# Moving the scaled down weights four steps earlier, the slot weight to VectorE, and swapping two waits in a fused attention and mixture-of-experts kernel

## The reference

```python
mod = (silu(c) @ wmod).reshape(2, 6, 1, 256)          # sa, ca, ga, sb, cb, gb
ga, gb = sign(ga) * max(|ga|, 0.25), sign(gb) * max(|gb|, 0.25)
h = layernorm(x) * (1 + ca) + sa
q, k, v, u = split(h @ W_qkvu.T); q, k = silu(q), silu(k)
o = decayed_linear_attention(q, k, v)                 # 16 heads of 16, a decay for each head
x = x + ga * ((u * rmsnorm(o)) @ W_out.T)
h = layernorm(x) * (1 + cb) + sb
# feed-forward: a shared expert, and the best 2 of 8 experts for each row
out = (silu(h @ sh_gate.T) * (h @ sh_up.T)) @ sh_down.T
for e in range(8):
    out += ((silu(h @ ex_gate[e].T) * (h @ ex_up[e].T)) @ ex_down[e].T) * comb[:, e]
x = x + gb * out
```

## Time and profile before

| | us |
|---|---|
| median of 3 runs | 419.76 (419.39 to 420.69) |
| the profiled execution | 419.39 |
| its span | 417.6 |
| TensorE busy | 391.2 |
| VectorE busy | 295.8 |
| ScalarE busy | 273.0 |
| GpSimd busy | 192.9 |

### The profile page before, as it was taken

How to read it: one execution, slowest core, us unless ns; L and a number is a source line. 1 busy time by engine, 2 the same in 40 slices (tenths; PEclk the granted TensorE clock), 3 DMA queues, 4 the chain that set the end, 5 groups by cost and what they waited for, 6 DMA issues and landing times.

```text
span 417.6 us, 11545 instructions
## 1 busy us (share of the span) xinstructions
PE 391.2 (94%) x4071; PEld 288.5 (69%) x4096; DVE 295.8 (71%) x601; ACT 273.0 (65%) x541; POOL 192.9 (46%) x192
## 2 busy tenths in 40 slices
PE   7989998999889867999999999999999999999993
PEld 4655466788668767999965666666666666666892
DVE  6996478898698763789778677767767775555542
ACT  4688667566666437475657778778687856656640
POOL 1000006577767964113445555565665565564240
PEclk9999999999999989899999999999999999999998
DMA  7850020001930069962322243344334333433224
GB/s 268 314 85 17 0 103 2 2 27 23 357 142 28 17 241 312 291 203 31 77 64 66 39 64 65 53 60 68 53 54 64 59 58 53 70 60 44 34 27 113
DMA packets 26253, 38.70 MB, mean 93 GB/s; under 512 B 4996, under 2 KB 20340, under 8 KB 26072
## 3 DMA queue, kind: packets, MB, share of 16 engines
q1 hardware_dynamic: 16120, 25.53, 19.3%
q0 software_dynamic: 7488, 10.27, 15.8%
q10 hardware_dynamic: 2592, 2.18, 1.6%
HBM read 27.60 MB, written 10.36 MB: 91 GB/s over the span
## 4 chain that ended last, share of the span: by engine, by line
PE 63%; DVE 17%; issue 7%; ACT 6%; DMA 4%; ACTq 1%; DVEq 1%; SPq 0%; POOLq 0%
PE ps L1508 23%; PE ps L1546 14%; PE ps L1516 8%; PE ps L1336 5%; PE ps L1525 4%; DVE wx L946 4%; PE ps L1479 3%; DMA wx<-in_wexp 2%; DVE xres L1009 2%; DVE tmp L1023 1%; DVE st L1012 1%; PE ps L1322 1%; DMA tmp<-in_decay_tables 1%; DVE rs L1041 1%; DVE st L862 1%
## 5 line engine op out<-in xcount | busy, mean ns | idle before, releaser
L1508 PE MATMUL ps<-wx,tmp 128*128 (+1 forms) x448 | 103.0, 379 | 1.1
L540 POOL DMA_INDIRECT out<-tmp,dk x39 | 66.2, 1699 | 70.7 <-DMA out<-tmp,dk 57.5
L1546 PE MATMUL ps<-wx,tmp 128*128 (+1 forms) x660 | 80.9, 273 | 0.2 <-DVE tmp L1193 0.2
L774 ACT ACTIVATE tmp<-tmp 128x512 bf16<-128x512 f32 x55 | 34.6, 629 | 63.3 <-DVE tmp L1184 37.3
L1508 PEld LDWEIGHTS ps<-wx,tmp 128*128 128x128 bf16 x468 | 44.2, 98 | 46.0
L1546 PEld LDWEIGHTS ps<-wx,tmp 128*128 128x128 bf16 x660 | 63.8, 98 | 16.0 <-DVE tmp L1193 0.5
L533 POOL DMA_INDIRECT tmp<-h2rows,src_i x39 | 41.4, 1061 | 20.9 <-issue 9.8
L1516 PE MATMUL ps<-tmp,wx 128*128 128x128 bf16 x768 | 48.9, 225 | 1.5 <-ACT tmp L765 1.5
L1199 DVE SCALAR_TENSOR_TENSOR woutg<-modr,w_hl,woutg 128x256 f32<-128x256 f32 x39 | 18.9, 485 | 42.7 <-ACT woutg L783 42.7
L1516 PEld LDWEIGHTS ps<-tmp,wx 128*128 128x128 bf16 x768 | 46.6, 101 | 1.8 <-issue 1.7
L1193 DVE TENSOR_TENSOR tmp<-tmp 128x512 bf16<-128x512 f32 x55 | 38.7, 704 | 6.8 <-ACT tmp L774 6.6
(11 more groups left out here) (195 smaller groups left out, 704.6 us busy)
## 6 DMA issues: line engine op xcount, KB each, us to landing
wx<-in_wexp SPq DMA_DIRECT2D x27, 512.0 KB, 5.5
xres<-in_x SPq DMA_DIRECT2D x4, 512.0 KB, 8.2
h2rows<-h2s ACTq DMA_DIRECT2D x16, 128.0 KB, 3.6
out<-h2s SPq DMA_DIRECT2D x12, 128.0 KB
h2s<-in_wmod SPq DMA_DIRECT2D x1, 1024.0 KB, 9.3
wx<-decay_rows SPq DMA_DIRECT2D x16, 64.0 KB
modr<-mod_rows SPq DMA_DIRECT2D x1, 1024.0 KB, 4.7
wx<-in_wqkvu SPq DMA_DIRECT2D x1, 768.0 KB, 8.4
```

Of the source, the lines that this page charges most:

```text
L540: e.indirect_dma_start(t["out"], bass.IndirectOffsetOnAxis(ap=dst_i[:, j:j + 1], axis=0), yb[(NA + j) % 2], None, compute_op=ALU.add).then ...
L774: e.activation(hs[p][:, 0:FF], hf[p], ACT.Copy).then_inc(s["inner_high"], 1)
L1508: ins = e.matmul(ps[:, bank, :], xT[p][:, (2 * a + k) * P:(2 * a + k + 1) * P], wx[:, bass.ds(at_ + weights(part, w) + k * FF, FF)], start ...
L1546: ins = e.matmul(half(DOWN_BANKS[p], 0, D), inner[:, (KF * a + k) * P:(KF * a + k + 1) * P], wx[:, bass.ds(off, D)] if routed(f) else wx[: ...
```

## The change

Three things:

- The products of the down piece run at steps 10 to 13 instead of 14 to 17, the second batch's first (into the stage's first slot), then the first batch's in place. The splits of these two products are at steps 13 and 15 of ScalarE (low parts at 14 and 16 of VectorE) instead of 16 and 18 (17 and 19). The second batch's is now the third part and the first batch's the fourth, so that `down(0)` waits for all four low parts, and `down(1)` for none.
- `make_weight` leaves ScalarE. VectorE makes the slot weight in `take_rows`, right behind the copy of the turned rows.
- In `add_rows` the two waits stand in the other order.

```diff
--- before.py
+++ after.py
@@ -345,8 +345,8 @@
             return early_stage[:, stage * PIECE:(stage + 1) * PIECE], wx[:, at_[0]:at_[0] + PIECE], wx[:, at_[1]:at_[1] + PIECE]
 
         SHARED_PARTS = [shared_part(0, [SHARED_AT + weights(0, a) for a in range(2)]), shared_part(1, [SHARED_AT + weights(1, a) for a in range(2)]),
-                        shared_part(0, [SHARED_AT + weights(2, a) for a in range(2)]), shared_part(2, [SECOND_DOWN + a * PIECE for a in range(2)])]
-        SHARED_PARTS_AT = (9, 10, 16, 18)
+                        shared_part(0, [SECOND_DOWN + a * PIECE for a in range(2)]), shared_part(2, [SHARED_AT + weights(2, a) for a in range(2)])]
+        SHARED_PARTS_AT = (9, 10, 13, 15)
 
 
 
@@ -514,19 +514,19 @@
 
 
                 part = slice(part * PIECE // 2, (part + 1) * PIECE // 2)
-                down, other_ = early_stage[:, 2 * PIECE:3 * PIECE][:, part], early_stage[:, 0:PIECE][:, part]
-                if b == 0:
-                    e.wait_ge(s["shared_loaded"], 16 * NPIECE)
+                down, second = early_stage[:, 2 * PIECE:3 * PIECE][:, part], early_stage[:, 0:PIECE][:, part]
+                e.wait_ge(s["shared_loaded"], 16 * NPIECE)
+                if b == 1:
                     e.wait_ge(s["shared_low"], 1)
                 else:
-                    e.wait_ge(s["shared_scaled"], 2)
-                e.tensor_tensor((other_, down)[b].rearrange("p (k n) -> p k n", n=D), down.rearrange("p (k n) -> p k n", n=D),
+                    e.wait_ge(s["second_scaled"], 2)
+                e.tensor_tensor((down, second)[b].rearrange("p (k n) -> p k n", n=D), down.rearrange("p (k n) -> p k n", n=D),
                                 modr[:, b, 3:4, :].to_broadcast([P, KF // 2, D]), ALU.mult).then_inc(s[("shared_scaled", "second_scaled")[b]], 1)
 
             for n in range(N_IT):
                 step_attention(n)
-                if 14 <= n < 18:
-                    scale_down((n - 14) // 2, n % 2)
+                if 10 <= n < 14:
+                    scale_down(1 - (n - 10) // 2, n % 2)
 
             def gather(j):
                 wait(e, "weight_made", j - 1)
@@ -535,8 +535,8 @@
 
             def add_rows(j):
 
+                wait(e, "result_made", j + 1)
                 wait(e, "rows_added", 16 * j)
-                wait(e, "result_made", j + 1)
                 e.indirect_dma_start(t["out"], bass.IndirectOffsetOnAxis(ap=dst_i[:, j:j + 1], axis=0),
                                      yb[(NA + j) % 2], None, compute_op=ALU.add).then_inc(s["rows_added"], 16)
 
@@ -696,9 +696,9 @@
                     whole_, high, _ = SHARED_PARTS[SHARED_PARTS_AT.index(n)]
                     e.wait_ge(s["shared_loaded"], 16 * NPIECE)
                     if n == SHARED_PARTS_AT[2]:
+                        e.wait_ge(s["second_scaled"], 2)
+                    if n == SHARED_PARTS_AT[3]:
                         e.wait_ge(s["shared_scaled"], 2)
-                    if n == SHARED_PARTS_AT[3]:
-                        e.wait_ge(s["second_scaled"], 2)
                     e.activation(high, whole_, ACT.Copy).then_inc(s["shared_high"], 1)
                 if mine(l):
                     tile = tile_of(l)[0]
@@ -745,17 +745,6 @@
                     wait(e, "inner_turned", f - NA + 1)
                     wait(e, "down_product", f - 1)
                     e.activation(hsT[f % 2], ps[:, FREE_BANK, :].bitcast(bf16), ACT.Copy).then_inc(s["inner_taken"], 1)
-
-            def make_weight(f):
-
-                if is_tile(f) and routed(f):
-                    j = f - NA
-                    wait(e, "rows_turned", f + 1)
-                    if j == 0:
-                        e.wait_ge(s["routing"], RT_COLUMNS + 4)
-                    w = xg[f % 2][:, D:].bitcast(f32)
-                    e.activation(slot_w[:, j:j + 1], w[:, 1:2], ACT.Identity, scale=second[:, j:j + 1],
-                                 bias=w[:, 0:1]).then_inc(s["weight_made"], 1)
 
             def middle(f):
                 if is_tile(f):
@@ -821,7 +810,6 @@
             f = N_IT - NT - 1
             middle(f - 1)
             for f in range(f, NF + 3):
-                make_weight(f + 1)
                 take_inner(f - 2)
                 take_rows(f + 1)
                 if f == MARK_AT:
@@ -1172,6 +1160,11 @@
                     wait(e, "up_product", f - 1)
                     e.tensor_copy(xT[f % 2].bitcast(u32), half(ROW_BANK, 0, D).bitcast(u32)).then_inc(s["rows_taken"], 1)
 
+                    j = f - NA
+                    w = xg[f % 2][:, D:].bitcast(f32)
+                    e.scalar_tensor_tensor(out=slot_w[:, j:j + 1], in0=w[:, 1:2], scalar=second[:, j:j + 1], in1=w[:, 0:1],
+                                           op0=ALU.mult, op1=ALU.add).then_inc(s["weight_made"], 1)
+
             def make_inner(f):
                 if is_tile(f):
                     p = f % 2
@@ -1535,8 +1528,8 @@
                         e.wait_ge(s["expert_low"], NPIECE)
                 else:
                     wait(e, "inner_low", f + 1)
-                    if f < B:
-                        e.wait_ge(s["shared_low"], NPIECE + f)
+                    if f == 0:
+                        e.wait_ge(s["shared_low"], NPIECE + 1)
                 down_free(e, f)
                 for n in range(3 * KF):
                     k, (a, w) = n // 3, PASSES[n % 3]
```

## The result

The changed kernel takes 424.2 us (median of 9 runs, 422.62 to 426.1), the kernel before beside it 420.38 (9 runs, 418.76 to 422.29): ratio 1.0093, 95% interval [1.0064, 1.012]. It is about 0.9% slower. The forecast was 418.7 with a range of 416.0 to 421.5; the time lies outside.

The account below looks back on a forecast made before the run. TensorE was taken as the bound in the routed tiles, the hand-over from attention as the place to gain. 0.4 - 0.6 - 0.8 + 0 = -1.0 us gave 418.4, or 418.7 us as median; range 416.0 to 421.5.

Parts of the forecast that it names:

- Part C: Swapping the two waits of add_rows before the 39 chained adds: nothing, between -0.1 and +0.5 us.
- A: Shared down weights' products and splits four steps earlier in attention: net +0.4 us, between -2.0 and +3.4.
- the clock: TensorE's granted clock at the hand-over from attention to shared tiles: -0.6 us taken, bounds 0 and -3.4.
- three terms: Work added in steps 10 to 16: GpSimd lateness 1.6, products meeting L1041 0.6, copies and differences 2.1; 4.3 us.
- the meetings: GpSimd products (L523) and VectorE's L1041 excluding each other: 1.08 and 0.94 us removed in steps 15 and 16, 0.6 added.
- the copies: Two ScalarE copies leaving TensorE's path, in step 16 and at 161.45 us: 0.95 us gained each.
- Rival 3: Clock stays up over the hand-over: 2.5 us more gain than taken, near 416.2 us; chance 0.22.
- B at the first routed tiles: Near 221 us, slot weight off ScalarE lets L1193 run before the gather: -0.8 us, bounds -0.93 and +0.6.
- B in the steady ring: VectorE–ScalarE ring of the expert tiles: 39 added operations at 0.08 us each, covered by 0.40 us per four tiles; cost nothing.
- Rival 1: Ring of the expert tiles becomes the bound, deciding at 0.10 us per weight; 421.5 us at 0.2 us; chance 0.14.
- Part B: Slot weight moved from ScalarE to VectorE: free in steady tiles unless 0.21 us or more each, -0.8 us at the first.
- The shape of the end: Last two adds with the waits swapped: the next to last gains about 0.5 us, the last loses 0.5.

Follow-up runs that it names:

- A and B: Kernel before with down products and splits moved earlier and the slot weight made on VectorE, add_rows waits in their old order: 417.48 us, ratio 0.9939.
- A only: Kernel before with only the down weights' products moved to steps 10 to 13 and their splits to 13 and 15: 416.85 us, ratio 0.9914.
- products alone: Kernel before with the four GpSimd products at steps 10 to 13, the splits left where they were: 418.56 us, ratio 0.9943.
- filled idle: Kernel before with ten unused matmuls of 512 columns put where TensorE idled 2.75 us at the hand-over: 420.16 us, ratio 0.9988.
- A and B with the weight in the gap: Kernel before with down products and splits earlier, old wait order, slot weight on VectorE behind L1184, where VectorE waits for ScalarE: 417.06 us, ratio 0.9921.
- double weight: Kernel before with the slot weight made on VectorE, and the same operation once more into columns nobody reads: 424.61 us, ratio 1.0091.
- B alone: Kernel before with only the slot weight moved from ScalarE to VectorE, behind the copy of the turned rows: 420.81 us, ratio 1.001.

## Why the prediction was wrong

The step that failed is **Part C**, "Nothing, between -0.1 and +0.5". It had the mechanism right (the wait first in the text is the one to which the DMA reacts fast; 0.76 us against 0.24) and asked the wrong question of it. It looked at the last two adds of the kernel, where one gains 0.5 and one loses 0.5, and not at the 37 before them. In the changed kernel the landing of the add before is what ends the wait of 36 of the 39. For those the term is a period: transfer 3.87 plus reaction 0.75 is 4.62 us, against TensorE's 4.57. It was over the threshold, and no rival priced it. Measured: +5.5 us alone, +6.5 on top of A and B.

Point by point:

- **A, +0.4 us, range -2.0 to +3.4; with the clock -0.2.** Measured -3.6. The distances of L1006 (L994) from step to step, from the one at 111.90 us on (before) and its counterpart, show where, in us:

| | 1 | 2 | 3 | 4 | 5 | 6 | 7 | 8 |
|---|---|---|---|---|---|---|---|---|
| before | 6.24 | 5.86 | 5.29 | 5.29 | 5.03 | 6.28 | 6.23 | 6.54 |
| A only | 6.24 | 6.39 | 5.67 | 6.71 | 5.20 | 5.90 | 4.34 | 4.91 |
| products alone | 6.24 | 6.38 | 5.67 | 5.76 | 5.48 | 5.20 | 5.29 | 5.13 |
| filled idle | 6.24 | 5.87 | 5.28 | 5.29 | 5.02 | 6.28 | 6.23 | 5.84 |

What the work adds in its new steps is 2.5 us (columns 2 to 5: 0.53, 0.38, 1.42, 0.17), where the prediction summed 4.3 from three terms; 1.8 of it are the products. What it gives back in its old ones is 3.9 us (columns 6 to 8), and 2.4 more from the last residual to the first down: 6.3 where 4.5 was forecast (2.0 for the meetings, 1.9 for the copies, 0.6 for the clock). The clock is 0.7 us of column 8, as the kernel with the filled idle shows, which has that gain and no other, and 1.4 of the 2.4. So 4.2 us are meetings and copies, near the forecast 3.9. Two terms were mis-sized, to the same side: the added work by 1.8 us and the clock by 1.5. The prediction said "the work meets the same neighbours a little earlier"; in fact the same work cost 2.5 us in the middle steps and 4.2 in the last ones, where TensorE, ScalarE and the shared tiles' start all stand in a queue. VectorE's wait in step 7 shows it, 2.25 us for ScalarE before and 0.16 with A (a row of before, then of A alone):

```profile
152.12 0.16 DVE L1006 RECIPROCAL rs<-rs 128x1 f32<-128x1 f32 x1 [2.25 <-ACT rs L662]
```

```profile
154.37 0.17 DVE L1006 RECIPROCAL rs<-rs 128x1 f32<-128x1 f32 x1 [0.16 <-ACT rs L662]
```

- **The meetings.** Foreseen: products meet L1041 (now L1029) in steps 11 and 13, 1.08 us each at most. In the changed kernel the worst L1029 there is 0.66 us long, and one product met L1035 and held it at 1.73 us, itself 2.27 us long. Engines that shut each other out are there, as the Trainium skill says ("SBUF — State Buffer", "Who interferes with whom"), but by that rule alone the move would have been an even trade, and it was not: meetings of 1.08 and 0.94 us went, new ones of 0.50 (L1029) and 0.51 (L1035, 1.22 undisturbed) came.

```profile
136.70 0.66 DVE L1029 SCALAR_TENSOR_TENSOR rs<-mv,rs 128x1 f32<-128x1 f32 x1
```

```profile
125.33 2.27 POOL L523 TENSOR_TENSOR wx<-wx,modr 128x512 f32<-128x512 f32 x1
```

- **The clock.** Rival 3 (it stays up, 0.22) came true. With the 0.6 of the sum it had 3.1 us for it; the rows show 2.1, 0.7 at the first fall and 1.4 at the second. Its reason, shorter idles, is not borne out for the second fall: the products alone kept the clock behind the 1.53 us of before.
- **B at the first routed tiles, -0.8 us.** Right: 51.05 to 50.10 us alone and 51.16 to 50.20 beside A. The wait for L1186 is gone, and the gather starts behind it:

```profile
217.88 0.21 DVE L1165 SCALAR_TENSOR_TENSOR dk<-tmp,dk 128x1 f32<-128x1 f32 x1
218.01 0.68 DVE L1186 TENSOR_TENSOR tmp<-tmp 128x512 bf16<-128x512 f32 x1
```

```profile
218.36 1.17 POOL L533 DMA_INDIRECT tmp<-h2rows,src_i  x1 [2.50 <-DVE dk L1165]
```

- **B in the steady ring, nothing.** Wrong by size: 0.13 us each where 0.08 was taken. Rival 1 had the threshold at 0.10, Part B itself at 0.21; 0.10 was the right number. That is rival 1 in its small form, +1.5 us. The 0.08 was no bad reading: L1041, one column too, takes 0.08 ahead of L1047 in the trace of before (122.46 to 122.54). It has a constant as scalar, the slot weight takes its scalar from SBUF; whether that is the difference no run shows.
- **The shape of the end.** The next to last add did not gain: it waits for a landing now. The last three adds of the changed kernel are 4.60 and 4.48 us apart, behind 2.9 to 3.1 us of waiting for the transfer before, and the last starts 12.6 us behind the last routed inner turn, not 11.1:

```profile
399.08 1.55 POOL L540 DMA_INDIRECT out<-tmp,dk  x1 [2.95 <-DMA out<-tmp,dk]
403.68 1.55 POOL L540 DMA_INDIRECT out<-tmp,dk  x1 [3.05 <-DMA out<-tmp,dk]
408.16 1.55 POOL L540 DMA_INDIRECT out<-tmp,dk  x1 [2.93 <-DMA out<-tmp,dk]
```

In sum, from the medians: A -3.6, B +0.4 (not told from nothing), together -2.6 (A and B measured at 0.9939), the swap +6.5: +3.9, measured +3.9 (0.0093 x 420.38). This sum closes by construction, since the swap's 6.5 is the difference of the two kernels. (The forecast's own sum gives 418.76, so 418.8 and not 418.7 as rounded.) What stays open is why the second fall of the clock went with the products' move, and whether the swap truly costs 1 us more beside A and B than alone.

Two kernels tried here beat both the kernel before and the changed one: A alone (416.85) and A and B with the weight in the gap (417.06), which the intervals do not tell apart.

## What to carry to other kernels

An edit that changes how fast an instruction reacts is priced against the period of the chain that it repeats in, not at its last link: add transfer, reaction and issue, and compare with the bound's period. Where several waits guard one instruction, put the one that comes last in the steady state first in the text, and put no idle wait in front of it. An operation of a tenth of a microsecond in a ring with 0.1 us of cover belongs into a place where its engine waits (here the traces show that gain, the time does not), and work that stands ahead of a hand-over between stages has less cover there than in the middle of a stage.

## What the runs showed of the hardware

- Of several waits ahead of a DMA that GpSimd issues, the first in the text is in the instruction and the others are instructions of their own on its queue. Behind one of these the DMA starts 0.75 us after the event (347.37 to 348.12), behind the first 0.24 us after it. A satisfied third wait costs as much as a wrong order, within the intervals (1.0102 and 1.0131).
- A one-column scalar_tensor_tensor of VectorE with its scalar from SBUF and no wait takes 0.13 us of its row (279.27 to 279.40, and between the two of the double weight); the profile shows it as 0.21 us long. One with a constant scalar takes 0.08 (122.46 to 122.54 in the kernel before) and is shown as 0.16.
- The granted clock fell behind an idle of 1.53 us once (before, 165.04 us) and of 1.53 again (the filled idle, 166.56 us), and behind 2.75 us (before, 152.08 us). It stayed at 1.00 behind idles of 1.00, 1.38 and 1.80 us, and also of 1.53 (the products alone, 165.20 us) and 2.76 (B alone, 153.09 us). So the length of the idle ahead does not decide it by itself in these traces.
